# One block of the second MLP product moved ahead of the next group's first convolution

## The reference, cut to what matters

```python
# layer 0, per graph: x (256 x 128)
h = relu(bn(conv1d(xc, conv1_w, 0)))            # width 1: "conv1"
h = bn(conv1d(h, conv2_w, 8))                   # width 17: the tap products
x_conv = relu(h + xc).T
s = x @ w_se.T + b_se
A = exp(-(|s_i|^2 + |s_j|^2 - 2 s s.T)) * mask
x_nmp = A @ relu(x @ w_msg.T + b_msg)
gi = concat(x_conv, x_nmp) @ w_ih.T + b_ih;  gh = x @ w_hh.T + b_hh
r = sigmoid(gi_r + gh_r); z = sigmoid(gi_z + gh_z); n = tanh(gi_n + r * gh_n)
x = layernorm(x + (1 - z) * n + z * x)
# layer 1
h = (1 + eps) * x + adj @ x
h = relu(h @ W1 + b1)                           # "mlp1" and hidden
x = layernorm(x + (h @ W2 + b2))                # "mlp2" and out_stats, out_norm
```

## Time and profile before

| what | value |
|---|---|
| median of 3 runs | 396.47 us |
| the profiled execution | 396.53 us |
| its span, first to last instruction | 394.7 us |
| PE matmul busy | 366.0 us (93%) |
| PE weight load busy | 319.3 us (81%) |
| DVE busy | 318.2 us (81%) |
| ACT busy | 230.8 us (58%) |
| POOL busy | 226.1 us (57%) |
| mean granted TensorE clock | 0.982 of full |
| data moved by DMA | 19.39 MB, mean 49 GB/s |

### The profile page before, as it was taken

The page is one execution under the profiler, slowest core; times in us unless marked ns, Lnnn a source line. Parts: engine busy times, 40 slices in busy tenths (PEclk is TensorE's granted clock), DMA queues, the critical chain, the costliest instruction groups (busy, mean ns, idle before and its releaser), DMA issues.

```text
span 394.7 us, 6487 instructions
## 1 busy us (share of the span) xinstructions
PE 366.0 (93%) x2191; PEld 319.3 (81%) x2191; DVE 318.2 (81%) x669; ACT 230.8 (58%) x423; POOL 226.1 (57%) x195
## 2 busy tenths in 40 slices
PE   2969795999999999999999999999999999999974
PEld 1848784979888898979888898979988898988954
DVE  4899879599588986999688986999778976986564
ACT  3535454373676567673676567574675557472773
POOL 3659362298437863497437963397436963395343
PEclk9999898799999999999999999999999999999998
DMA  6500000430101300120101201130101301000011
GB/s 231 216 0 1 2 2 1 159 109 1 55 4 49 108 29 27 55 106 0 53 0 53 106 14 39 53 106 2 53 2 53 108 2 55 1 2 0 2 53 53
DMA packets 7991, 19.39 MB, mean 49 GB/s; under 512 B 672, under 2 KB 5024, under 8 KB 6944
## 3 DMA queue, kind: packets, MB, share of 16 engines
q1 hardware_dynamic: 7536, 18.50, 13.4%
q10 hardware_dynamic: 432, 0.59, 0.4%
HBM read 14.90 MB, written 4.19 MB: 48 GB/s over the span
## 4 chain that ended last, share of the span: by engine, by line
PE 79%; DVE 12%; issue 3%; ACT 3%; DMA 2%; POOL 1%; SPq 0%; DVEq 0%; ACTq 0%; POOLq 0%
PE conv L1218 25%; PE back L1218 23%; PE front L1316 7%; PE back L1316 7%; PE back L1405 6%; DVE xl L821 5%; PE front L1288 2%; PE conv L1266 2%; PE back L1367 2%; DMA tail<-in_conv_dram 2%; PE front L1308 1%; ACT nmph L615 1%; PE conv L1288 1%; PE front L1298 1%; DVE wl L1042 1%
## 5 line engine op out<-in xcount | busy, mean ns | idle before, releaser
L1218 PE MATMUL conv<-sth,wh 128*128 128x256 f32 x238 | 74.6, 313 | 7.2 <-DVE wl L1042 4.6
L1218 PE MATMUL conv<-stl,wh 128*128 128x256 f32 x238 | 69.3, 291 | 0.0
L1218 PE MATMUL conv<-sth,wl 128*128 128x256 f32 x238 | 69.1, 290 | 0.0
L516 POOL TENSOR_TENSOR rstd<-rstd,minus_half 128x4 f32<-128x4 f32 (+1 forms) x34 | 38.8, 1141 | 38.2 <-DVE rstd L993 37.6
L1218 PEld LDWEIGHTS conv<-sth,wh 128*128 128x128 f32 x238 | 46.6, 196 | 11.2 <-DVE wl L1042 4.8
L521 POOL TENSOR_TENSOR xw<-xw,xv 128x512 f32<-128x512 f32 (+1 forms) x17 | 20.9, 1230 | 52.0 <-ACT xw L681 52.0
L534 POOL TENSOR_TENSOR amat<-amat,adjT 128x512 f32<-128x512 f32 x32 | 49.4, 1577 | 1.4 <-ACT amat L657 1.4
L1218 PEld LDWEIGHTS conv<-stl,wh 128*128 128x128 f32 x238 | 46.7, 196 | 0.3
L1218 PEld LDWEIGHTS conv<-sth,wl 128*128 128x128 f32 x238 | 46.5, 195 | 0.0
L615 ACT ACTIVATE sth<-sv 128x272 fp32r<-128x272 f32 (+1 forms) x35 | 18.2, 519 | 41.3 <-DVE sv L840 26.9
L528 POOL TENSOR_TENSOR tail<-xn,later_w 128x512 f32<-128x512 f32 (+1 forms) x17 | 29.8, 1756 | 4.3 <-DMA out_dram<-tail 2.6
(11 more groups left out here) (219 smaller groups left out, 1010.9 us busy)
## 6 DMA issues: line engine op xcount, KB each, us to landing
adjT<-in_adj_dram SPq DMA_DIRECT2D x8, 1024.0 KB, 4.8
out_dram<-tail SPq DMA_DIRECT2D x15, 256.0 KB, 2.2
xv<-in_x_dram SPq DMA_DIRECT2D x7, 512.0 KB, 3.3
gbuf<-in_gates_dram SPq DMA_DIRECT2D x1, 576.0 KB, 6.5
tail<-in_conv_dram ACTq DMA_DIRECT2D x2, 256.0 KB, 3.8
xv<-in_x_dram SPq DMA_DIRECT2D x2, 256.0 KB, 4.8
later_w<-in_later_dram SPq DMA_DIRECT2D x1, 452.0 KB, 6.9
tail<-in_conv_dram SPq DMA_DIRECT2D x1, 320.0 KB, 5.4
```

The source lines that it names most:

```text
L516: done(pool.tensor_tensor(rstd[:, k, h, q], rstd[:, k, h, q], minus_half[:, q], ALU.pow), RSTD[k])
L1218: ins = pe.matmul(bank, a, b, start=first and k == 0, stop=last and k == len(todo) - 1)
```

## The change

In PE's list of a round, mlp2(gb, 0) goes from behind the two conv1 blocks to ahead of them. mlp2(gb, 1) stays where it is. No instruction is added or taken away, no wait is changed, and no other engine's list is touched. In the last round, which has no conv1, the order is the same as before.

```diff
                 taps(gm, INF, 1, 2)
                 mlp1(gb, 0)
                 mlp1(gb, 1)
+                mlp2(gb, 0)
                 if front:
                     conv1(gf, ub, 0)
                     conv1(gf, ub, 1)
-                mlp2(gb, 0)
                 mlp2(gb, 1)
                 nmp(gm, 0)
                 taps(gm, INF, 2)
```

## The result

The changed kernel takes 398.89 us, the median of 17 runs (397.19 to 399.71), beside 396.56 us for the kernel before in 17 runs of the same comparison. The ratio is 1.0049, with a 95% interval of 1.0036 to 1.0062: slower by 1.9 us, between 1.4 and 2.5 (the two medians alone are 2.3 apart). The forecast was 397.5 with a range of 394.9 to 398.9, 0.36 on slower.

The account below looks back on a forecast made before the run. PE was taken to set the pace (busy 44.47 of 44.70 us a round). Winning 0.46 at conv1 and then waiting about 0.6 at PLUS2 gave +0.17 in six rounds, +1.0 on 396.5: 397.5 us, range 394.9 to 398.9.

Parts of the forecast that it names:

- Where the win was: PE's wait for xl ahead of conv1's second product goes away: 0.46 us a round, 2.8 us in six rounds.
- the switch between kinds of product: PE changes product kind once more per round; taken at nothing, bounded by 0.1 us either way.
- lost again at PLUS2: conv1 ends 1.33 us later, delaying ACT, POOL and DVE; PE then waits about 0.6 us at the third tap product.
- The slack of 0.83: Time in us between DVE's stream_low(2) being ready for PE (231.86) and PLUS2's weight load (232.69).
- The lateness of half_stream: On DVE, half_stream starts 0.90 to 1.17 us later, taken as 1.0, because xconv_low and POOL's token_diffs exclude each other.
- rival 3: DVE's xconv_low goes ahead of POOL's second token_diff: shift 1.17 or more, +0.34 a round, +2.0 us, 398.5; chance 0.32.
- rival 1: xconv_low and token_diffs do not exclude each other: half_stream shifts 0.56 to 0.81, total -1.2 us, 395.3; chance 0.17.
- The price of a round: Net change per round on PE, half_stream's shift of 1.0 less the slack of 0.83: +0.17 us.
- Six rounds: The six rounds with a conv1 each pay +0.17 us, +1.0 us in all; the seventh is unchanged.
- HALF: First tap product on PE: its input comes 0.1 us short, swallowed by the wait behind it.
- its own signs: Wrong if half_stream shifts under 0.8 us, PLUS2 doesn't wait, or PE waits anywhere else, at HALF above all.
- Rival 2: The later chain is not felt and PE's gap is simply won, needing a shift under 0.38: 393.7 us; chance 0.03.

Follow-up runs that it names:

- the two kernels that keep it: Kernel before with a quarter, then a half, of mlp2(gb, 0) between the two conv1: 394.62 us (ratio 0.9935) and 393.77 us (0.9915).
- the kernels with spare work: Kernel before with two, then four spare bn_stats ahead of half_stream on DVE: 396.78 us (ratio 0.9990) and 399.46 us (1.0065).
- the second sample: The changed kernel run once more, unaltered, beside the kernel before on the same chip: 398.58 us, ratio 1.0050.
- the kernel before against itself: The kernel before, unaltered, measured as if it were a changed one: 397.41 us, ratio 1.0012.

## Why the prediction was right and where it was off

- **Where the win was, and its size: right.** 0.46 us a round at xl; measured 0.49 on PE's way to nmp, and 0.44 to 0.50 in the two kernels that keep it. mlp2(0) did not wait for the hidden activations, and the switch between kinds of product cost nothing that the rows show.
- **That it is lost again at PLUS2, over ACT, POOL and DVE: right.** The first token_diff was put at 223.78 and started in step at 223.75. The slack of 0.83 was confirmed by the kernels with spare work. But the forecast put the likeliest result within 0.3% (0.47), and the kernel is slower by 0.36% to 0.62%, on which it had put 0.36.
- **The lateness of half_stream: 1.0 forecast, 1.07 measured,** inside the bounds of 0.90 to 1.17. The term that was off is who goes first at the end of the first token_diff. I took the middle between both orders; it was the order of rival 3, DVE ahead of POOL's waiting instruction, and with a lateness above the 1.03 from which it was to decide (though under its 1.17) and a time near its +2.0 us, rival 3 (chance 0.32) came nearer than the forecast (0.45). The forecast's other half, that DVE and POOL exclude each other there, held, so rival 1 fell: its lateness of 0.56 is what remains when xconv_low is taken away (0.54).
- **The price of a round: +0.17 forecast, +0.27 measured.** 0.07 of the miss is the term above. Another 0.03 comes in on the way: stream_low(2) is 1.10 late where half_stream is 1.07, and 1.10 - 0.83 is the 0.27.
- **Six rounds: right.** All six pay, round 1 with 0.32 us and the others with 0.25 to 0.32. Where the total was low, it was the price of a round and not the count: 1.0 forecast, 1.6 to 1.7 in the rounds.
- **The total: +1.0 forecast, +1.9 measured (1.4 to 2.5).** The 1.6 to 1.7 us of the rounds lie inside this interval and inside that of the second sample (1.2 to 2.7). The remaining 0.2 to 0.3 us are within the noise: the clock of the prologue and of round 1 moves single executions by more, and the kernel before against itself gave 1.0012 (0.9997 to 1.0028). The fastest executions of each, 395.86 and 397.19, are 1.3 apart; the six executions of the changed kernel with the highest mean granted clock (0.988 and 0.989) have spans of 395.4 to 396.1 us, mean 395.8, the 21 of the kernel before with its highest (0.990 and 0.991) have a mean of 394.4, 1.4 less.
- **That the time fell into the range is partly luck:** the median of 398.89 lies at its upper end of 398.9. The forecast of 397.5 stood on the 396.5 of three runs of the kernel before, whose 17 runs have 396.56, so the base was sound; the price was about half of what was measured.
- **HALF:** forecast 0.1 short and swallowed. Its weight load stood 0.24, and from the second nmp to its second product PE took 0.12 longer (230.79 - 228.83 against 229.27 - 227.43), which the wait at PLUS2 swallowed. By the letter of its own signs, which named a wait at HALF, this spoke against the forecast; by its working it was expected.

Rival 2 (393.7, the gap simply won) is the kernel with half a block: not this change, but a smaller dose of it.

## What to carry to other kernels

A gap of 0.46 us on the pacing engine is worth filling with 0.4 to 0.9 us of work (a quarter or a half of the block), not with 1.8: whatever is pushed back by the rest starts its own chain, and that chain's slack has to be measured link by link before the move. When an engine off the path is moved in time, look not only at who waits for it but at what now runs beside it: here xconv_low had begun just as POOL finished (225.28 against 225.34), and came to lie beside the next of POOL's instructions. Where only part of a block fits, split the block.

## What the runs showed of the hardware

- When POOL's first token_diff ended, two were waiting: DVE's small tensor_scalar with xconv_low behind it, and POOL's second token_diff. DVE ran both its instructions and POOL stood for about 0.53 us (1.87 instead of 1.34). With the masks it was the other way: POOL's next mask went ahead of the second xl. What decides the order at such a handover no run here shows.
- A tensor_scalar of 128x4 elements, 0.17 us alone, took 0.26 to 1.11 us when it came due during a token_diff (0.26 with three quarters of the block, 0.84 after the change, 1.11 with the half block), up to the end of the token_diff in each case. Small as it is, it stood as long as the rest of POOL's instruction took.
- The same prologue ran at a granted clock between 0.50 and 1.00 in the stretch from 23 to 28 us, after PE had been idle for 3.2 us, from one execution to another. The Trainium skill, TensorE: Matmul & The Clock Gate, Part 1, says that the slow stretch varies from run to run of the same kernel; the trace agrees, and in these profiles it moves the first messages by up to 1.4 us (49.22 against 50.61), nearly as much as the edit costs.
